# Storing the normalised tokens transposed through TensorE, and loading them plainly ahead of the router and the experts

## The reference

```python
xn = _layernorm(x, axis=-1)                       # x: (4, 4096, 2048) f32
s = _L0_attn_ref(xn, WQ, bQ, WK, bK, WV, bV, proj)
g = _silu(_L0_ffn_ref(xn, shared_w1, ..., centroids, bias))
x = x + s * g

# _L0_ffn_ref, d = 2048, d_ff = 1408, 2 shared and 16 routed experts, 4 of them weighted per token
h = relu(einsum('td,ndf->ntf', flat, shared_w1) + shared_b1[:, None, :])
out = flat + einsum('ntf,nfd->td', h, shared_w2) + shared_b2.sum(0)
scores = sigmoid(flat @ centroids.T) + bias
vals, idx = top_k(scores, 4)                      # gating: vals at idx, divided by their sum
# for every routed expert: out += (relu(flat @ w1 + b1) @ w2 + b2) * gating[:, e]
```

## Time and profile before

| | us |
|---|---|
| median of 2 runs | 8992.16 |
| the two runs | 8657.72 and 9326.6 |
| the profiled execution | 8646.81 |
| its span, slowest core (core 5) | 8645.3 |
| spans of the 8 cores | 8576.2 to 8645.3 |
| mean granted TensorE clock, all cores | 0.885 to 0.890 |

### The profile page before, as it was taken

The page is one execution under the profiler, slowest core; times in us unless marked ns, Lnnn a source line. Parts: engine busy times, 40 slices in busy tenths (PEclk is TensorE's granted clock), DMA queues, the critical chain, the costliest instruction groups (busy, mean ns, idle before and its releaser), DMA issues.

```text
span 8645.3 us, 79991 instructions; the slowest of 8 cores (8576.2 to 8645.3 us)
## 1 busy us (share of the span) xinstructions
PE 6657.3 (77%) x29264; PEld 2884.8 (33%) x29264; DVE 1648.1 (19%) x3424; ACT 936.3 (11%) x1217; POOL 623.8 (7%) x748
## 2 busy tenths in 40 slices
PE   0235556645589899999999994558999999999995
PEld 0112222212133344434434442213444444444442
DVE  3333332321011111111111112200112111121112
ACT  0132221100001100100010011000010100101011
POOL 0000000000011111111111110000000000000000
PEclk9956667777699999999999997768999999999997
DMA  4222220025577887888788787232222222222223
GB/s 147 84 97 76 81 78 28 15 54 102 141 127 127 138 147 129 136 147 141 124 138 146 130 138 180 68 120 92 71 84 72 74 82 70 80 72 82 79 65 135
DMA packets 1016250, 885.39 MB, mean 102 GB/s; under 512 B 502702, under 2 KB 908334, under 8 KB 1001408
## 3 DMA queue, kind: packets, MB, share of 16 engines
q0 software_dynamic: 552496, 354.08, 26.4%
q1 hardware_dynamic: 264752, 353.68, 12.6%
q10 hardware_dynamic: 198624, 172.52, 6.3%
HBM read 809.01 MB, written 266.34 MB: 124 GB/s over the span
## 4 chain that ended last, share of the span: by engine, by line
PE 68%; DMA 17%; DVE 6%; issue 4%; ACT 3%; POOL 1%; ACTq 1%; DVEq 0%; SPq 0%; POOLq 0%; PEldq 0%
PE psA L849 13%; PE psB L849 12%; PE psC L904 9%; PE psD L904 8%; PE psF L904 8%; PE psE L904 8%; DMA w1b<-rw 4%; DMA xlorl<-scr_qlo 3%; DMA w2b<-rw 3%; PE ptr L237 1%; DMA kxt<-xkv 1%; PE psC L620 1%; DMA xt<-xq 1%; DMA wstg<-wq 1%; DVE kst L364 1%
## 5 line engine op out<-in xcount | busy, mean ns | idle before, releaser
L849 PE MATMUL psA<-xnqTh,w1b 128*128 128x512 bf16 x6336 | 1462.3, 385 | 186.7 <-DMA w1b<-rw 146.6
L849 PE MATMUL psB<-xnqTh,w1b 128*128 128x512 bf16 x6336 | 1432.1, 379 | 0.0
L849 PEld LDWEIGHTS psA<-xnqTh,w1b 128*128 128x128 bf16 x6336 | 616.8, 99 | 990.9 <-issue 296.1
L904 PE MATMUL psC<-w2b,hT 128*128 128x512 bf16 x3168 | 777.8, 397 | 150.4 <-DMA xlorl<-scr_qlo 77.7
L849 PEld LDWEIGHTS psB<-xnqTh,w1b 128*128 128x128 bf16 x6336 | 620.1, 98 | 747.4
L904 PE MATMUL psF<-w2b,hT 128*128 128x512 bf16 x3168 | 764.0, 391 | 65.5 <-DMA xlorl<-scr_qlo 65.5
L904 PE MATMUL psD<-w2b,hT 128*128 128x512 bf16 x3168 | 764.7, 392 | 64.1 <-DMA xlorl<-scr_qlo 64.1
L904 PE MATMUL psE<-w2b,hT 128*128 128x512 bf16 x3168 | 764.0, 391 | 63.5 <-DMA xlorl<-scr_qlo 63.5
L935 DVE SCALAR_TENSOR_TENSOR acc<-psC,gating,acc 128x512 f32<-128x512 f32 x256 | 192.2, 751 | 3143.9 <-PE psC L904 3143.9
L855 ACT ACTIVATE hT<-psA,rb_sb 128x512 bf16<-128x512 f32 x352 | 241.8, 687 | 3702.9 <-PE psA L849 3605.1
L904 PEld LDWEIGHTS psC<-w2b,hT 128*128 128x128 bf16 x3168 | 316.7, 101 | 568.4 <-issue 229.7
(11 more groups left out here) (189 smaller groups left out, 2914.8 us busy)
## 6 DMA issues: line engine op xcount, KB each, us to landing
scr_w<-w1b ACTq DMA_DIRECT2D x198, 512.0 KB, 3.8
w1b<-rw POOLq DMA_DIRECT2D x352, 256.0 KB, 7.1
w1b<-scr_w POOLq DMA_DIRECT2D x108, 512.0 KB, 3.7
scr_w<-w2b SPq DMA_DIRECT2D x72, 704.0 KB, 6.9
scr_w<-w2b ACTq DMA_DIRECT2D x72, 704.0 KB, 8.5
w2b<-scr_w SPq DMA_DIRECT2D x72, 704.0 KB, 5.7
w2b<-scr_w POOLq DMA_DIRECT2D x72, 704.0 KB, 7.2
w2b<-rw POOLq DMA_DIRECT2D x64, 768.0 KB, 9.9
```

The lines of the kernel that those rows point to most:

```text
L849: ins = e.matmul(ps[:, :], wb[:, dc, :], xnqTh[:, dc, sub * 512:(sub + 1) * 512], start=(dc == 0), stop=(dc == NDC - 1))
L904: ins = e.matmul(ps[:, :], hT[:, fs, tt * 128:(tt + 1) * 128], w2b[:, fs, qb, :], start=(fs == 0), stop=(fs == NFC - 1 and not extras))
```

## The change

Two DRAM tensors scr_qT and scr_qloT are added, which hold hib and lob transposed: 2048 rows (features) by 2048 tokens, bf16. In the Q stretch:

- after the 16 transposes of a tile's hib, its part of the window xnWq is stored to scr_qT on dY, waiting for the 16 copies: 128 partitions by 16 chunks by 128 tokens, thus runs of 256 B in DRAM rows of 4096 B;
- then lob is transposed the same way through `TRP`, copied by DVE into loT (two buffers), and stored to scr_qloT on dY, waiting for these 16 copies;
- the copies into xnWq wait for the store of the same part of the window four tiles ago; the copies into loT wait for the store two tiles ago; the next user of lob waits for its transposes;
- xfb has one buffer in place of two.

The stores to scr_q and scr_qlo stay, since the experts' first pass reads them. Ahead of the router, the DMA transposes into xnqTh and lowin on dS become plain loads from scr_qT and scr_qloT, even chunks on dY and odd ones on dS, each 128 rows of 2048 B, waiting for all transposed stores.

```diff
--- before.py
+++ after.py
@@ -172,6 +172,8 @@
     scr_q = ap(nc.dram_tensor("scr_q", [TQ, D], BF16, kind=dscr))
     scr_qlo = ap(nc.dram_tensor("scr_qlo", [TQ, D], BF16, kind="Internal"))
     s_scr = ap(nc.dram_tensor("s_scr", [TQ, D], BF16, kind=dscr))
+    scr_qT = ap(nc.dram_tensor("scr_qT", [NDC * 128, TQ], BF16, kind="Internal"))
+    scr_qloT = ap(nc.dram_tensor("scr_qloT", [NDC * 128, TQ], BF16, kind="Internal"))
     scr_w1 = ap(nc.dram_tensor("scr_w1", [18, NFC, 128, NDC * 128], BF16, kind="Internal"))
     scr_w2 = ap(nc.dram_tensor("scr_w2", [18, 8, 128, NFC * 256], BF16, kind="Internal"))
     out = ap(nc.dram_tensor("out", [TQ, D], F32, kind="ExternalOutput"))
@@ -349,8 +351,12 @@
         stats = [A2("st0", [128, 8]), A2("st1", [128, 8])]
         hib = [A2("hib0", [128, D], BF16), A2("hib1", [128, D], BF16)]
         lob = [A2("lob0", [128, D], BF16), A2("lob1", [128, D], BF16)]
-        xfb = [A2("xfb0", [128, D]), A2("xfb1", [128, D])]
+        xfb = [None, None]
+        xfb_s = A2("xfb", [128, D])
+        xfb[0] = xfb_s
+        xfb[1] = xfb_s
         xnWq = A2("xnWq", [128, NDC, 1, 512], BF16)
+        loT = [A2("loT0", [128, NDC, 128], BF16), A2("loT1", [128, NDC, 128], BF16)]
 
         def ln_tile(bufs, src_ap, row0, b, want_lo, prevu, dst_scr, prev_lo):
             xt, stats, hib, lob, xfb = bufs
@@ -404,6 +410,10 @@
         qwin_users = [[], []]
         pq_ev = [None, None]
         qev_all = []
+        hiT_stores = []
+        loT_stores = []
+        prev_hiT_store = [None] * 4
+        prev_loT_store = [None, None]
         for tc in range(4):
             w = 0
             evs_this = []
@@ -414,18 +424,45 @@
                 q_hi.append(hs)
                 q_lo.append(ls)
                 hb = hib[k % 2]
+                lob_b = lob[k % 2]
+                lo_st = lou[1] if lou else None
                 tsts = []
+                tile_evs = []
                 for dc in range(NDC):
                     def mkev(pap, tst, dc=dc, w=w, kk=kk):
                         return S.op("V", lambda e, pap=pap, dc=dc, w=w, kk=kk: e.tensor_copy(
                             xnWq[:, dc, w, kk * 128:(kk + 1) * 128], pap),
-                            deps=[tst] + qwin_users[w])
+                            deps=[tst] + qwin_users[w] + [prev_hiT_store[kk]])
                     tst, ev = TRP(hb[:, dc * 128:(dc + 1) * 128], 128, 128, ident[:, :],
                                   mkev, [hi_st, ld_ident])
                     tsts.append(tst)
                     evs_this.append(ev)
+                    tile_evs.append(ev)
+                hst = S.dma("dY", lambda e, k=k, kk=kk: e.dma_start(
+                    scr_qT[0:2048, 128 * k:128 * (k + 1)]
+                    .rearrange("(dc p) t -> p dc t", p=128),
+                    xnWq[:, :, 0, kk * 128:(kk + 1) * 128]), deps=tile_evs)
+                prev_hiT_store[kk] = hst
+                hiT_stores.append(hst)
+                lo_tsts = []
+                lo_evs = []
+                for dc in range(NDC):
+                    def mklo(pap, tst, dc=dc, k=k):
+                        return S.op("V", lambda e, pap=pap, dc=dc, k=k: e.tensor_copy(
+                            loT[k % 2][:, dc, :], pap),
+                            deps=[tst, prev_loT_store[k % 2]])
+                    tst, ev = TRP(lob_b[:, dc * 128:(dc + 1) * 128], 128, 128, ident[:, :],
+                                  mklo, [lo_st, ld_ident])
+                    lo_tsts.append(tst)
+                    lo_evs.append(ev)
+                lst = S.dma("dY", lambda e, k=k: e.dma_start(
+                    scr_qloT[0:2048, 128 * k:128 * (k + 1)]
+                    .rearrange("(dc p) t -> p dc t", p=128),
+                    loT[k % 2][:, :, :]), deps=lo_evs)
+                prev_loT_store[k % 2] = lst
+                loT_stores.append(lst)
                 prevu[k % 2] = lu + [tsts[-1]]
-                prev_lo[k % 2] = lou
+                prev_lo[k % 2] = lou + [lo_tsts[-1]]
             users = []
             for a in range(4):
                 g = a % 2
@@ -712,16 +749,16 @@
             hoff = half * HALF
             trh = []
             for dc in range(NDC):
-                t = DMT("dS", xnqTh[:, dc, :],
-                        scr_q[hoff:hoff + HALF, dc * 128:(dc + 1) * 128],
-                        deps=q_hi + U["xnqTh"])
+                t = DMA(("dY", "dS")[dc % 2], xnqTh[:, dc, :],
+                        scr_qT[dc * 128:(dc + 1) * 128, hoff:hoff + HALF],
+                        deps=hiT_stores + U["xnqTh"])
                 trh.append(t)
 
             rt_steps = []
             for dc in range(NDC):
-                tl = DMT("dS", lowin[:, dc % 2, :],
-                         scr_qlo[hoff:hoff + HALF, dc * 128:(dc + 1) * 128],
-                         deps=q_lo + [U["lowin"][dc % 2]])
+                tl = DMA(("dY", "dS")[dc % 2], lowin[:, dc % 2, :],
+                         scr_qloT[dc * 128:(dc + 1) * 128, hoff:hoff + HALF],
+                         deps=loT_stores + [U["lowin"][dc % 2]])
 
                 def rtfn(e, dc=dc):
                     for sub in range(2):
```

## The result

| | before | changed |
|---|---|---|
| median | 9338.26 us (10 runs) | 9305.87 us (11 runs) |
| lowest and highest | 8652.35, 9609.27 | 8774.0, 9736.5 |
| ratio of the undisturbed runs | | 1.017, 95% interval 1.0098 to 1.0241 |
| span of the slowest core in the profile | 8645.3 us | 8816.5 us |

Most runs of either kernel are disturbed: some or all cores show a lower mean granted TensorE clock (down to 0.77, where it is 0.88 to 0.89 otherwise), and the run takes 9017 to 9737 us here whatever the kernel; the ratio leaves those out, the medians do not. The forecast was +138 us, 1.6%. The predicted time, 8785 us in a range of 8735 to 8870, was missed all the same, since the median of the changed kernel's runs lies at 9306.

What follows compares the result with a forecast made beforehand. The prediction took the Q stretch as bound by a serial ring through SP's issue order; 149 us for inner turns, 24 across Q matmuls and -35 for the loads gave +138 on 8646.8, 8785 us, range 8735 to 8870.

Steps and rivals of the forecast that it cites:

- Sum: Last step for the whole kernel: 149 + 24 - 35 = +138 us on the profiled run's 8646.8, giving 8785 us.
- The signs: Trace marks expected: Q turns some 31 us, 39 across Q matmuls, barrier about 2008, first router step 21 us later.
- P: Q stretch: time one new transposed store of 2048 runs of 256 B takes; taken as 4.4 us.
- Bound of the Q stretch, and SP's order: Q stretch: serial ring, 18.8 us per token tile, since SP's program order puts the next load behind the stores.
- Term (a): Q stretch: 256 PE transposes and DVE copies of lob, 5.9 us per tile.
- Term (b): Q stretch: two stores delay the next load; from lob store's issue (L), landed L+20.3 instead of 7.9, +12.4 us per turn.
- (c): Q stretch: one xfb buffer instead of two costs nothing.
- (d), (e): Ahead of the experts: plain loads of xnqTh (d) and lowin (e) replace DMA transposes, together -35 us.
- Rival 1: Q stretch: short stores are slow, P from 6.7 up; +189 us at 7.3, +218 at 8.5; chance 0.27.
- Rival 2: Ahead of the experts: the loads bring nothing, Q cost as forecast; +173 us, 8820; chance 0.13.
- Rival 3: Q stretch and loads all at the cheap end: P = 3.1 and 73 us saved; +84, 8731; chance 0.06.
- Rival 4: Q stretch: the next load is not held behind the stores; -11 us, at best -49; chance 0.02.

Runs made afterwards that it cites:

- Experiments 4: Changed kernel with the two transposed stores of each tile on POOL's queue instead of SP's: Q stretch 732.3 us, ratio 1.0102 to the kernel before.
- experiment 6: Changed kernel with each xt load put ahead of the previous tile's stores, all on SP: Q stretch 731.3 us.
- experiment 5: Changed kernel with each tile's transposed lo store issued a second time, to an unread tensor: Q stretch ends at 858.9 us, 27 to 29 more.
- experiment 3: Kernel before with plain loads into xnqTh and lowin, taken untransposed: the four stages with loads and router steps 34.3 us shorter, Q stretch as before.
- experiment 7: Changed kernel with hib, lob and khib transposed eight at a time, one DVE copy each: Q stretch 715.1 us, 116.6 less than the changed kernel.
- 10: The change on top of the kernel before with early loads and transposes eight at a time: ratio 0.9664 to the kernel before.

## Why the prediction was right in its sum and wrong in its time

**The step that failed is the one under "Sum".** It took the profiled run's 8646.8 us as the level of the answer and set the upper of the two runs aside as "one run of 9326.6, about which the profile says nothing". Ten runs of the kernel before have their median at 9338: the run set aside stood for most of them. The profile could not tell why, but the two times did tell that the kernel has two levels, half of the known runs on each. A range for the time had to reach from 8735 to about 9326.6 + 138 = 9465, or the forecast had to be made as a difference, for which +138 us was close: on the lower level the four shortest of the changed kernel's eleven runs took 8774 to 8855 us. No mechanism had to be found for that; one of two numbers had to be taken at its word. Why there is an upper level stays open: no experiment here bears on it, and both kernels have it.

Point by point:

- **The signs: met but for one.** Inner turns 30.3 us (31 forecast), across the Q matmuls 38.5 (39), the loads ahead of the router from 1994.9 (2008), the first router step 20.5 us later (21), the expert rows within 0.3% (0.5). Only the landing of the transposed stores is off, 3.8 and 4.2 us for 5.5; that is P, below.
- **Bound of the Q stretch, and SP's order: right.** Experiments 4 and 6 move the load out from behind the stores in two ways and both bring 22 us turns, 732 and 731 us.
- **Term (a), 5.9 us for 16 transposes and copies: right** (L + 5.4 to L + 11.4). Across the Q matmuls a turn grew by about 5.5 us, 5.9 forecast.
- **Term (b), P = 4.4: mis-sized.** By experiment 5 the store costs 2.2 us in its place (2.4 on the mean of the cores), below the low end of 3.1 that I took from packets of DMA transposes and cast loads at 169 GB/s; neither was a row of plain stores. The centf row, the w1b row and the 156 GB/s row led even further up. The turn came out at +11.4 instead of +12.4: with P = 2.2 the formula gives 11.8 + 2.2 + 4.1 - 7.9 = 10.2. Of the missing 1.2 us 0.2 are the load's issue, at L + 12.0; the other 1.0 lies between its issue and its landing, 7.3 us where the formula with P = 2.2 has 6.3. What makes it up is not shown. So the size of P was off by half and an unforeseen 1.2 us hid part of that, which was luck. The Q stretch: +173 forecast, +159 on the profiled core, +164 on the mean.
- **(c) one xfb buffer at nothing: right** as long as the load stands behind the copies; once it was put ahead, the kernel needed a wait for lob there (experiment 6).
- **(d), (e) the loads, -35: right in size**, 35.8 in the changed kernel and 34.3 alone (experiment 3). By part: 15.4 and 9.9 for the loads (11 and 12 forecast), 4.5 and 6.0 for the turns (5 and 7). The ground for (d) was only half of it: I priced the transposes by the engines' 169 GB/s, but the chain before goes through ACT's issues of them, 30.5 us for 16. Where an issue takes 1.30 us, 256 KB at a time, that is about 200 GB/s by itself, not far from the measured pace. The issues of 2.8 to 3.9 us fall beside the first w1b loads, so there the engines may have held the issue back. For lowin the issue went from 1.16 to 0.33 us, which covers the whole difference in landing, 3.3 to 2.6 or 2.7.
- **Rival 1, slow short stores: fell.** The Trainium skill's rule on transfers below 512 B (DMA: Bandwidth & Descriptors, "Specifications") may say rightly what the engine does; a doubled time is not seen here. 512 KB in 2.2 to 2.4 us are about 220 to 240 GB/s, against 315 for the plain tiles of the earlier trace rows.
- **Rival 2, no gain from the loads: fell** by the stages of experiment 3 and of the changed kernel. By the Trainium skill's rule (Advanced Engine Details and Errata, "X-Bar Transpose (TRN2)") transposes are as fast; here the same bytes came 14 us sooner as plain loads. Whether the transposing transfers themselves are slower, or only their issue, no run shows.
- **Rival 3, all at the cheap end: fell** in its sum, +84. The loads save 35.8 us and not 73; its P of 3.1 was nearer to the measured 2.2 than mine.
- **Rival 4, the load not held: fell** (it was issued at L + 12.0). It describes experiments 4 and 6. Its chance of 0.02 was counted under "faster by over 2%", which its own -11 to -49 us rule out.
- **A row misread:** the expert halves do not run "at the full clock"; the earlier trace rows has 0.95 for both. Nothing of the sum rests on it.

## What to carry to other kernels

A DMA put on a queue costs first of all what stands behind it there; look at which load is next in the issuing engine's order before pricing the bytes. A load that is issued ahead of the previous tile's stores, and transposes that share one PSUM copy, were together worth twice what the change cost, with no new data path. And when the times shown lie far apart, forecast a difference, and let a range for the time itself cover every level that the runs show.

## What the runs showed of the hardware that I had not expected

- DVE's copy out of PSUM in bf16 takes 0.22 us for 128 columns and 0.69 us for 1024 (experiment 7); I had expected 1.2 for the latter.
- A DMA transpose of 256 KB holds ACT for 1.16 to 1.30 us at its issue where nothing holds it up, a plain load of 256 KB for 0.33 (kernel before and changed kernel).
- A store of 2048 runs of 256 B takes 2.2 to 2.4 us between others (experiment 5), and the issue of the DMA behind it on SP was longer the more was queued, in the rows shown: 0.68, 1.15 and 2.79 us behind none, one and two such stores (experiments 4, the changed kernel, 5). Behind stores that follow each other closely it was 2.1 to 2.6 (experiments 7 and 10).
